# First stage of a fused adaLN, gated delta rule and mixture-of-experts block: groups pipelined, modulation rows spread by TensorE, first weights loaded there

## The chip, the cores and the metric

One core of a Trainium2 chip runs the whole program in one launch. The metric is device time in microseconds, the median of a few runs; smaller is better.

## The reference, cut to what matters

```python
mod = (silu(c) @ wmod).reshape(8, 6, 1, 256)           # sa, ca, ga, sb, cb, gb
h = layernorm(x) * (1 + ca) + sa                       # x: 8 x 256 x 256
x = x + ga * attn(h)                                   # gated delta rule, 32 heads
x = x + gb * ffn(layernorm(x) * (1 + cb) + sb)         # 8 experts, 2 of them per token, and a shared one
# inside attn, first lines:
h = rmsnorm(h, rms1_w)
g = -exp(A_log) * softplus(h @ Wa + dt_bias)           # decay of each head and token
beta = sigmoid(h @ Wb)
q, k, v = conv+silu of h @ Wq, h @ Wk, h @ Wv
```

`ga` and `gb` are kept at least 0.25 away from zero, sign kept. Everything is float32 at the boundaries.

## The kernel before

The program has three parts, one after the other, each a block of its own that all engines enter and leave together: `prepare` (the first stage), `delta_rule` (64 turns, one per batch and group of four heads, software-pipelined by a table of pieces called `PLAN`), and the experts. The change touches `prepare` and the start of `delta_rule`.

**`prepare`.** The 2048 tokens are 16 tiles of 128 rows, in 4 groups of 4 tiles (`GROUPS`, `GT`). SyncE issues all loads (L186 to L196). When every small load has landed (one semaphore, `ld`), ScalarE takes silu of `c`, TensorE makes all six modulation rows for the 8 batches (L221: 6 matmuls, `p_wmod`), VectorE copies them out of PSUM (L293), adds 1 to the scales and bounds the gates (L295 to L303). SyncE stores the rows to memory (L200) and loads two of them back, each copied to all 128 partitions (L202, `p_modb`). VectorE waits for that load and for all of `x`, and then `turn(g)` runs for the four groups in a loop, on all engines in step: mean and variance (L310, L313), the power of -1/2 on GpSimd (L254), centring (L318), times scale and plus shift (L324, into `acc`), squares and their sums on ScalarE (L267), mean of squares, again a power on GpSimd (L256), scaling into `p_hn` (L335), eight transposes on TensorE (L229), and two copies on ScalarE into `hT` (L271), which `delta_rule` reads. VectorE goes to group g+1 only after it has scaled group g.

After the loop TensorE multiplies all of `hT` by `Wa` and `Wb` (L239, 16 matmuls; the four groups write four different ranges of 32 partitions), and a chain of VectorE and ScalarE instructions on tiles of 128 x 512 makes decay and beta: bias (L343), softplus by a series (L344 to L355), the product with exp(A_log) (L357), exp (L281), the reciprocal for beta (L361), running products (L365), a memset (L368). SyncE stores decays (L206) and products (L210) and waits until they have landed; then the stage ends.

**`delta_rule`, start.** SyncE loads `Wo` (L477) and `gnorm_w` (L478), waits for five memsets of VectorE and GpSimd (`set_ok`; L841 to L843, L1003 to L1005), loads the first weights (L487 to L496) and then the tiles of the first two turns: `dr_hb` (L524), `dr_abc` (L525), `dr_bcb` (L528). TensorE waits for `Wo`, the weights and `dr_hb`, and starts with the projections (L593). From there on the table sets the order on every engine.

Of the kernel before, what the change touches and what calls it, by code (L numbers as in the profile page):

```python
# [140 lines left out]

def prepare(nc, A, mem, scr):

    with ExitStack() as ctx:
# [4 lines left out]
        modb = sb("modb", [P, B, 2 * D])  # L149
# [4 lines left out]
        sgn = sb("sgn", [B, 6 * D])  # L154
# [17 lines left out]
        ld, ldx, mod_st, modb_ld, scr_st = (sem(n) for n in ("ld", "ldx", "mod_st", "modb_ld", "scr_st"))
        c_silu, mod_ps, mod_ok = (sem(n) for n in ("c_silu", "mod_ps", "mod_ok"))
        dve, half_ok = (sem(n) for n in ("dve", "half_ok"))
        var_ok, rstd_ok, h0_ok, ss_ok, ms_ok, rr_ok, hn_ok, tr_ps, ht_ok = (
            sem(n) for n in ("var_ok", "rstd_ok", "h0_ok", "ss_ok", "ms_ok", "rr_ok", "hn_ok", "tr_ps", "ht_ok"))
        z_ps, absz_ok, u_ok, sp_ok, a_ok, az_ok, eb_ok, beta_ok, bt_ps, bcum_ok = (
            sem(n) for n in ("z_ps", "absz_ok", "u_ok", "sp_ok", "a_ok", "az_ok", "eb_ok", "beta_ok", "bt_ps", "bcum_ok"))
        acts, done, late, passed, passed_pool = (sem(n) for n in ("acts", "done", "late", "passed", "passed_pool"))
        NLD = 1 + 1 + 2 + 1 + 2 * GROUPS + 1  # L180
# [4 lines left out]
        def _(sp):  # L185
            sp.dma_start(mem["const"][:], A["consts"]).then_inc(ld, 16)  # L186
            sp.dma_start(ct[:], A["c"]).then_inc(ld, 16)
            sp.dma_start(wmod[:], A["wmod"].rearrange("(k p) n -> p k n", k=KT)).then_inc(ld, 16)
            sp.dma_start(wab[:, :, 0:H], A["Wa"].rearrange("(k p) n -> p k n", k=KT)).then_inc(ld, 16)
            sp.dma_start(wab[:, :, H:2 * H], A["Wb"].rearrange("(k p) n -> p k n", k=KT)).then_inc(ld, 16)  # L190
            sp.dma_start(w1c[:], A["rms1_w"]).then_inc(ld, 16)
            for g in range(GROUPS):
                sp.dma_start(dtb[H * g:H * (g + 1), :], A["dt_bias"].rearrange("(h a) -> h a", a=1)).then_inc(ld, 16)
                sp.dma_start(alog[H * g:H * (g + 1), :], A["A_log"].rearrange("(h a) -> h a", a=1)).then_inc(ld, 16)
            for g in range(GROUPS):
                sp.dma_start(x1[:, g * GT:(g + 1) * GT, :],  # L196
                             A["x"].rearrange("b (c p) d -> p (b c) d", p=P)[:, g * GT:(g + 1) * GT, :]).then_inc(ldx, 16)
# [6 lines left out]
            sp.wait_ge(az_ok, 1)  # L204
            for g in range(GROUPS):
# [1275 lines left out]
```

## Time and profile before

| | us |
|---|---|
| median of 3 runs | 2630.22 |
| lowest, highest | 2629.96, 2634.56 |
| the profiled execution, its own time | 2633.98 |
| its span | 2632.2 |

Busy shares of the span: TensorE 94% (weight loads beside it 78%), VectorE 78%, ScalarE 64%, GpSimd 34%. The mean clock granted to TensorE is 0.967 of full speed. The busy share in 40 equal slices (65.8 us each), TensorE above, the granted clock below:

```
PE   1289999999999999999999999999999999789997
PEclk6589999999999999999999999999999999889998
```

A 9 is 90% or more. The profile gives all times from the span's start; names that begin with `p_` belong to `prepare`, with `dr_` to `delta_rule`.

### The profile page before, as it was taken

The numbers are of one execution on the slowest core, as the hardware profiler recorded it, in microseconds if no ns is written. First come the engines' busy times: TensorE is split into PE (matmuls) and PEld (weight loads), VectorE is DVE, ScalarE is ACT, GpSimd is POOL, SyncE is SP. The second block draws the span as 40 slices with busy tenths as digits, with TensorE's granted clock in tenths as the row PEclk, the third lists the DMA queues.
The fourth block names the chain that finished last, engine by engine and source line by source line (L and its number), as shares of the span: only waits on it lengthen the run. The fifth ranks groups of instructions, "written<-read, shape, count | busy, mean of one in ns | idle before, by whom it ended". The sixth has DMA issues, their size and how long they took to land. (4 is left out here: it accounts for less than half of the span.)

```text
span 2632.2 us, 59594 instructions
## 1 busy us (share of the span) xinstructions
PE 2466.6 (94%) x21984; PEld 2063.6 (78%) x21984; DVE 2057.6 (78%) x4303; ACT 1689.0 (64%) x3890; POOL 899.0 (34%) x1053
## 2 busy tenths in 40 slices
PE   1289999999999999999999999999999999789997
PEld 0168888888888888888888888888888888646655
DVE  3468888888888888888888888888888888535444
ACT  1157777777777777777777777777777777522221
POOL 0033444444444444444444444444444444100000
PEclk6589999999999999999999999999999999889998
DMA  2221121112111211121112111121112110031000
GB/s 98 86 57 40 41 60 42 41 41 60 42 41 42 60 41 41 42 60 41 42 41 56 45 42 41 52 49 42 41 45 56 41 42 14 1 121 32 33 6 11
DMA packets 148317, 120.45 MB, mean 46 GB/s; under 512 B 24305, under 2 KB 128698, under 8 KB 148034
## 3 DMA queue, kind: packets, MB, share of 16 engines
q1 hardware_dynamic: 148034, 116.66, 16.7%
q8 instruction: 180, 2.95, 0.5%
q14 instruction: 103, 0.84, 0.1%
HBM read 72.11 MB, written 2.54 MB: 28 GB/s over the span
## 5 line engine op out<-in xcount | busy, mean ns | idle before, releaser
L740 DVE TENSOR_TENSOR dr_w<-dr_ps,mask 128x512 bf16<-128x512 f32 x768 | 526.3, 685 | 90.5 <-PE dr_ps L556 89.7
L754 DVE SCALAR_TENSOR_TENSOR dr_y<-dr_ps,dr_cw,dr_y 128x255 f32<-128x255 f32 (+2 forms) x1152 | 475.8, 474 | 38.1 <-ACT dr_y L870 38.1
L856 ACT CAST dr_tn<-dr_ps 128x512 bf16<-128x512 f32 x640 | 375.0, 586 | 157.6 <-PE dr_ps L569 156.7
L859 ACT CAST dr_tt<-dr_ps 128x512 bf16<-128x512 f32 x768 | 459.2, 598 | 20.9 <-PE dr_ps L576 20.9
L653 PE MATMUL dr_ps<-dr_w,dr_am 128*128 128x96 f32 x3072 | 418.2, 279 | 9.5 <-ACT dr_w L916 2.1
L653 PEld LDWEIGHTS dr_ps<-dr_w,dr_am 128*128 128x128 f32 x3072 | 378.8, 193 | 32.3 <-ACT dr_w L916 24.5
L870 ACT ACTIVATE dr_y<-dr_ps,dr_cw 128x256 f32<-128x256 f32 x384 | 160.9, 470 | 222.2 <-PE dr_ps L593 222.1
L576 PE MATMUL dr_ps<-dr_tt,dr_w 128*128 128x128 bf16 x3072 | 297.6, 219 | 0.9 <-DVE dr_w L740 0.9
L556 PE MATMUL dr_ps<-dr_tn,dr_b 128*128 128x128 bf16 x3072 | 297.6, 219 | 0.0
L982 POOL TENSOR_SCALAR_AFFINE_SELECT dr_b<-dr_b 128x512 bf16<-128x512 bf16 x128 | 81.6, 637 | 506.9 <-ACT dr_b L906 506.9
L569 PEld LDWEIGHTS dr_ps<-dr_w,dr_tt 128*128 128x128 bf16 x2560 | 186.7, 101 | 84.5 <-issue 49.3
L569 PE MATMUL dr_ps<-dr_w,dr_tt 128*128 128x128 bf16 x2560 | 248.5, 220 | 4.2 <-DVE dr_w L740 3.2
L969 POOL TENSOR_TENSOR dr_dg<-const,dr_gam 128x512 f32<-128x512 f32 x128 | 130.4, 1039 | 335.0 <-DVE dr_gam L781 335.0
L916 ACT COPY dr_w<-dr_ps 128x384 f32<-128x384 f32 x384 | 190.0, 495 | 56.8 <-PE dr_ps L653 56.7
L593 PE MATMUL dr_ps<-dr_hb,dr_wqk 128*128 128x256 f32 x768 | 197.0, 393 | 21.1 <-DMA dr_hb<-hT 21.1
L961 POOL TENSOR_TENSOR dr_sq<-dr_sy 128x256 f32<-128x256 f32 x128 | 75.7, 612 | 390.8 <-ACT dr_sy L884 390.8
L576 PEld LDWEIGHTS dr_ps<-dr_tt,dr_w 128*128 128x128 bf16 x3072 | 203.5, 98 | 1.5 <-DVE dr_w L740 1.4
L556 PEld LDWEIGHTS dr_ps<-dr_tn,dr_b 128*128 128x128 bf16 x3072 | 204.4, 98 | 0.0
L719 PE MATMUL dr_ps<-dr_wo,dr_oT 128*128 128x256 f32 x768 | 196.7, 393 | 1.0 <-ACT dr_oT L942 1.0
L614 PE MATMUL dr_ps<-dr_wg,dr_hb 128*128 128x384 f32 x512 | 193.6, 501 | 0.6 <-ACT dr_gs L896 0.6
L789 DVE TENSOR_TENSOR dr_am<-dr_ps,dr_dec 128x512 f32<-128x512 f32 x256 | 174.8, 684 | 24.6 <-PE dr_ps L636 24.5
L766 DVE TENSOR_TENSOR_SCAN dr_dec<-dr_abc,dr_dg 128x512 f32<-128x512 f32 x128 | 191.0, 1492 | 1.3 <-POOL dr_dg L969 1.2
(188 smaller groups left out, 4784.2 us busy)
## 6 DMA issues: line engine op xcount, KB each, us to landing
dr_abc<-scr_a SPq DMA_DIRECT2D x64, 512.0 KB, 5.6
dr_qk<-dr_sy SPq DMA_DIRECT2D x384, 48.0 KB, 2.0
dr_hb<-hT SPq DMA_DIRECT2D x64, 256.0 KB, 2.5
dr_bcb<-scr_b SPq DMA_DIRECT2D x128, 64.0 KB, 4.7
dr_qk<-dr_sy SPq DMA_DIRECT2D x128, 32.0 KB, 1.9
ex_modb<-scr_mod SPq DMA_DIRECT2D x4, 1024.0 KB, 8.2
dr_wo<-in_Wo SPq DMA_DIRECT2D x1, 3072.0 KB, 10.9
dr_wv<-in_Wv SPq DMA_DIRECT2D x8, 384.0 KB, 4.0
```

The costliest lines, as they stand in the source:

```text
L556: last = pe.matmul(ps[:, (X0, X1)[g], (u % QH) * P:(u % QH + 1) * P], b16[:, m, u, :], id16[:] if l == 0 else tn[:, u, :], start=True, sto ...
L569: last = pe.matmul(ps[:, (X2, X1)[g], (u % QH) * P:(u % QH + 1) * P], tt[:, u, :], w16[:, u, :], start=True, stop=True)
L576: last = pe.matmul(ps[:, (X0, X2)[g], (u % QH) * P:(u % QH + 1) * P], wt[:, u, :], id16[:] if l == 0 else tt[:, u, :], start=True, stop=True)
L593: last = pe.matmul(ps[:, BANK[n], j * T:(j + 1) * T], wt, hb[:, m, k, :], start=(k == 0), stop=(k == KT - 1))
L614: last = pe.matmul(ps[:, A0, 0:QV], hb[:, m, k, c * P:(c + 1) * P], wg[:, k, :], start=(k == 0), stop=(k == KT - 1))
L653: last = pe.matmul(ps[:, bank, h * DV:(h + 1) * DV], wt(h), x[:, h * DV:(h + 1) * DV], start=(start and h == 0), stop=(h == QH - 1), skip_ ...
L719: last = pe.matmul(ps[:, CO, 0:D], oT[:, t, :], wo[:, (it // B) * VT + t, :], start=(t == 0), stop=(t == VT - 1))
L740: v.tensor_tensor((tn if l == 0 else w16)[:, us, :], ps[:, (X0, X1)[g], :].rearrange("p (u n) -> p u n", u=QH), bc(mask[:, l, :], 1, QH), ...
L754: v.scalar_tensor_tensor(y[:, slot, x:T], ps[:, BANK[n], off:off + T - x], cw[:, t, TAPS - 1 - x:TAPS - x], y[:, slot, x:T], ALU.mult, ALU ...
L766: v.tensor_tensor_scan(flat(dec[:, us, :]), flat(abc[:, m, c]), flat(dg[:, us, :]), 0.0, ALU.mult, ALU.add).then_inc(s["dec_ok"], 1)
L856: act.copy(tn[:, us, :], ps[:, (X2, X1)[g], :].rearrange("p (u n) -> p u n", u=QH)).then_inc(s["tn_ok"], 1)
L859: act.copy(dst, ps[:, (X0, X2)[g], :].rearrange("p (u n) -> p u n", u=QH)).then_inc(s["tt_ok"], 1)
```

## The change

In `prepare`:

- SyncE loads `c` and the first third of `wmod` first, then `x` (a semaphore for each group), then the constants of the stage, the rest of `wmod`, the first turn's weights (a new function `load_weights`), `gnorm_w` and `Wo`. Those tiles and their semaphores now live for the whole program. At the stage's end it stores decays, products, and last the modulation rows.
- TensorE makes only the first two modulation rows at first (2 matmuls). `spread(b)` copies the two rows of batch b to all partitions by a matmul of a one-hot column with the 8 x 512 rows, into one of three PSUM banks; VectorE multiplies and adds straight from there. The store and the load back are gone from the start.
- The centring moves from VectorE to ScalarE (`center`, Identity with scale and bias; GpSimd makes the bias by one more product). GpSimd scales two of a group's four tiles, VectorE the other two. The squares wait for one another.
- The groups are written out, each engine in an order of its own: VectorE takes the statistics of group g+2 before it is done with group g. `Wa` and `Wb` follow each group (4 matmuls) in place of 16 at the end.
- The other four modulation rows are made after the last group, the gates bounded at the very end on VectorE; the reciprocal for beta comes after the running products.

In `delta_rule` SyncE issues neither weights nor `Wo`: after `set_ok` its first transfer is `dr_hb`. The pieces keep their order on every engine.

```diff
 @block.sync
-            sp.dma_start(mem["const"][:], A["consts"]).then_inc(ld, 16)
-            sp.dma_start(ct[:], A["c"]).then_inc(ld, 16)
-            sp.dma_start(wmod[:], A["wmod"].rearrange("(k p) n -> p k n", k=KT)).then_inc(ld, 16)
+            sp.dma_start(ct[:], A["c"]).then_inc(s["c_ld"], 16)
+            sp.dma_start(wmod[:, :, 0:2 * D], w_v[:, :, 0:2 * D]).then_inc(s["c_ld"], 16)
...
+            sp.dma_start(wmod[:, :, 2 * D:], w_v[:, :, 2 * D:]).then_inc(s["m_ld"], 16)
+            load_weights(sp, A, mem, 0)
+            sp.dma_start(mem["gw"][:], A["gnorm_w"]).then_inc(mem["c_ld"], 16)
+            sp.dma_start(mem["wo"][:], A["Wo"].rearrange("(t p) n -> p t n", p=P)).then_inc(mem["c_ld"], 16)
-            sp.wait_ge(mod_ok, 2)
-            sp.dma_start(scr["mod"], mod[:]).then_inc(mod_st, 16)
-            sp.wait_ge(mod_st, 16)
-            sp.dma_start(modb[:], scr["mod"][:, 0:2 * D].partition_broadcast(P)).then_inc(modb_ld, 16)
...
+            sp.wait_ge(s["mod_ok"], 2)
+            sp.dma_start(scr["mod"], mod[:]).then_inc(s["mod_st"], 16)
+            sp.wait_ge(s["mod_st"], 16)
+            sp.wait_ge(mem["scr_st"], 2 * GROUPS * 16)
 @block.tensor
+            def spread(b):
+                wait(pe, s["bc_free"], b - NBC + 1)
+                pe.matmul(ps[:, BC + b % NBC, :], bc(const[0:B, C_ID + b], 1, P), mod[:, 0:2 * D],
+                          start=True, stop=True).then_inc(s["bc_ps"], 1)
...
+            for g in range(GROUPS):
+                turn(g)
+                steps(g)
+                for b in (2 * g + 4, 2 * g + 5):
+                    if b < B:
+                        spread(b)
 @block.vector
+            stats(0)
+            stats(1)
+            modulate(0)
+            stats(2)
+            means(0)
+            modulate(1)
+            scaled(0)
...
 delta_rule, @block.sync
-            sp.dma_start(wo[:], A["Wo"].rearrange("(t p) n -> p t n", p=P)).then_inc(s["c_ld"], 16)
-            sp.dma_start(gw[:], A["gnorm_w"]).then_inc(s["c_ld"], 16)
-
             sp.wait_ge(s["set_ok"], 5)
+            sp.wait_ge(s["scr_st"], 16 * 2 * GROUPS)
...
-            weights(0)
             batch(0, 0)
             batch(0, 1)
```

TensorE in `prepare`, before. `p_wmod` are the modulation matmuls, `p_hn` the transposes, `p_wab` the products with `Wa` and `Wb`:

```order
L221 MATMUL p_ps<-p_wmod,p_cs 8x512 x6
L229 MATMUL p_ps<-const,p_hn 128x128 x8
...
L229 MATMUL p_ps<-const,p_hn 128x128 x8
L105 REGISTER_ALU
L105 COMPARE_AND_BRANCH
L239 MATMUL p_ps<-hT,p_wab 32x512 x16
L244 MATMUL p_ps<-const,p_t_b 128x128 x4
```

And with the change, where `p_mod,const` are the spreads:

```order
L227 MATMUL p_ps<-p_wmod,p_cs 8x512 x2
L233 MATMUL p_ps<-p_mod,const 128x512 x4
L242 MATMUL p_ps<-const,p_hn 128x128 x8
L250 MATMUL p_ps<-hT,p_wab 32x512 x4
L233 MATMUL p_ps<-p_mod,const 128x512 x2
...
L242 MATMUL p_ps<-const,p_hn 128x128 x8
L250 MATMUL p_ps<-hT,p_wab 32x512 x4
L227 MATMUL p_ps<-p_wmod,p_cs 8x512 x4
L274 MATMUL p_ps<-const,p_t_b 128x128 x4
```

The 16 matmuls of `p_wab` are now four sets of 4, each behind its group's transposes, and eight spreads lie between the groups.

SyncE at the start of `delta_rule`, before:

```order
L477 DMA dr_wo<-in_Wo 128x24x256
L478 DMA dr_gw<-in_gnorm_w 128x3
L487 DMA dr_wqk<-in_Wq 128x2x192
...
L496 DMA dr_cw<-in_conv_v_w 128x3x4
L524 DMA dr_hb<-hT 128x2x256
L525 DMA dr_abc<-scr_a 128x2x512
```

And with the change, from the end of `prepare`:

```order
L210 DMA scr_a<-p_t_a 32x4x128 x4
L215 DMA scr_b<-p_t_bc 32x2x128 x4
L219 DMA scr_mod<-p_mod 8x1536
L153 UNCONDITIONAL_BRANCH
L557 UNCONDITIONAL_BRANCH
L593 DMA dr_hb<-hT 128x2x256
L594 DMA dr_abc<-scr_a 128x2x512
```

Eleven transfers have left the place between the two stages, and the store of the modulation rows has come to the end of the first.

## Rows read from the trace of the kernel before

**Rows 1.** Busy time by stretches: first stage, the gap, the rest.
```profile
0.00:112.94 112.94, 21.87 (x80) 9.52 (x80) 54.41 (x131) 17.04 (x47) 8.36 (x13) 0.63 0.18 61
112.94:128.58 15.64, 0.00 (x0) 0.03 (x1) 1.30 (x3) 0.00 (x0) 0.18 (x3) 0.50 0.98 316
128.58:2632.20 2503.62, 2444.75 (x21904) 2054.07 (x21904) 2001.93 (x4169) 1671.97 (x3843) 890.44 (x1037) 0.99 0.17 43
```

The columns are: stretch, its length, busy time and instructions of PE, PEld, DVE, ACT, POOL, granted clock, DMA share, GB/s.

**Rows 2.** Timeline up to the first group (start, length, engine, line).
```profile
11.87 7.36 PE L221 MATMUL p_ps<-p_wmod,p_cs 128*8 128x512 f32 x12 [11.87 <-ACT p_cs L263]
...
24.28 0.35 SPq L200 DMA_DIRECT2D scr_mod<-p_mod  x1
26.38 0.38 SPq L202 DMA_DIRECT2D p_modb<-scr_mod  x1
33.24 1.41 DVE L310 BATCH_NORM_STATS2 p_st<-p_x 128x6 f32<-128x256 f32 x4 [8.99 <-DMA p_modb<-scr_mod]
```

**Rows 3.** Timeline of the second group and the start of the third.
```profile
44.70 1.40 DVE L310 BATCH_NORM_STATS2 p_st<-p_x 128x6 f32 x4
...
49.69 2.73 DVE L324 TENSOR_TENSOR acc<-acc,p_modb  x4 [0.17 <-DVE acc L318]
52.55 0.42 ACT L267 ACTIVATE p_sq<-acc 128x256 f32 x1 [5.02 <-DVE acc L324]
...
55.68 1.14 DVE L335 TENSOR_SCALAR p_hn<-acc,p_rr 128x256 f32 x4 [1.22 <-POOL p_rr L256]
56.73 1.40 DVE L310 BATCH_NORM_STATS2 p_st<-p_x 128x6 f32 x4
```

**Rows 4.** Busy time by stretches, as rows 1, around TensorE's bursts.
```profile
20.00:44.00 24.00, 0.00 (x0) 0.00 (x0) 10.50 (x31) 1.70 (x8) 2.02 (x2) 0.56 0.24 89
80.00:84.00 4.00, 2.08 (x12) 1.69 (x16) 0.91 (x4) 1.53 (x3) 0.00 (x0) 0.50 0.00 0
87.00:90.00 3.00, 2.41 (x20) 0.48 (x15) 1.97 (x4) 0.85 (x2) 0.00 (x0) 0.88 0.00 0
```

**Rows 5.** Timeline, the last transposes and the products with `Wa` and `Wb`.
```profile
81.04 1.96 PE L229 MATMUL p_ps<-const,p_hn 128*128 128x128 f32 x8 [10.09 <-DVE p_hn L335]
...
83.88 5.53 PE L239 MATMUL p_ps<-hT,p_wab 128*32 128x512 f32 x32 [0.87 <-ACT hT L271]
```

**Rows 6.** Timeline of the first stage's end.
```profile
87.64 0.75 DVE L343 TENSOR_SCALAR p_t_z<-p_ps,p_dtb 128x512 f32<-128x512 f32 x1 [6.73 <-PE p_ps L239]
...
102.97 3.35 DVE L361 RECIPROCAL p_t_b<-p_t_q 128x512 f32<-128x512 f32 x1
106.24 1.31 DVE L365 TENSOR_TENSOR_SCAN p_t_bc<-p_t_a,p_t_zero 128x128 f32<-128x128 f32 x4
...
112.94 0.10 POOL L1003 MEMSET dr_half<- 128x8 f32 x1 [33.21 <-POOLq L144]
```

**Rows 7.** Timeline of the gap between the stages.
```profile
113.39 4.98 SPq L478 DMA_DIRECT2D dr_gw<-in_gnorm_w  x1
...
114.50 0.06 DVE L843 MEMSET dr_mso<- 128x4 f32 x1
...
124.53 0.71 SPq L524 DMA_DIRECT2D dr_hb<-hT  x1
...
128.58 4.56 PE L593 MATMUL dr_ps<-dr_hb,dr_wqk 128*128 128x256 f32 x12 [21.09 <-DMA dr_hb<-hT]
...
136.63 3.92 SPq L509 DMA_DIRECT2D dr_qk<-dr_sy  x6
```

**Rows 8.** DMA issues up to 120 us: size, median us from issue to landing.
```profile
const<-in_consts SPq DMA_DIRECT2D x1, 528.0 KB, 3.5
```

**Rows 9.** The page's DMA issues, the same columns.
```profile
dr_abc<-scr_a SPq DMA_DIRECT2D x64, 512.0 KB, 5.6
...
dr_hb<-hT SPq DMA_DIRECT2D x64, 256.0 KB, 2.5
```

**Rows 10.** The page's groups: GpSimd on a 128 x 256 tile.
```profile
L961 POOL TENSOR_TENSOR dr_sq<-dr_sy 128x256 f32<-128x256 f32 x128 | 75.7, 612 | 390.8 <-ACT dr_sy L884 390.8
```

More of the change, by code:

```diff
@@ L216, in _, with modulation @@
         def _(pe):
-            pe.wait_ge(ld, 16 * NLD + 0)
-            pe.wait_ge(c_silu, 1)
-            for n in range(3):
+            def modulation(n, bank):
                 for k in range(KT):
-                    last = pe.matmul(ps[0:B, n, :], cs[:, k, :], wmod[:, k, n * 512:(n + 1) * 512],
+                    last = pe.matmul(ps[0:B, bank, :], cs[:, k, :], wmod[:, k, n * 512:(n + 1) * 512],
                                      start=(k == 0), stop=(k == KT - 1))
-            last.then_inc(mod_ps, 1)
+                return last
@@ L242, in _, with steps @@
-            pe.wait_ge(beta_ok, 1)
+                        last = pe.transpose(ps[:, TR + k, j * P:(j + 1) * P], hn[:, g % 2, j, k * P:(k + 1) * P],
+                                            const[:, C_ID:C_ID + P])
+                    last.then_inc(s["tr_ps"], 1)
+            def steps(g):
+                pe.wait_ge(s["ht_ok"], (g + 1) * KT)
+                for w in range(2):
+                    for k in range(KT):
+                        last = pe.matmul(ps[H * g:H * (g + 1), (ZA, ZB)[w], :], wab[:, k, H * w:H * (w + 1)],
+                                         hT[:, k, g * GTOK:(g + 1) * GTOK], start=(k == 0), stop=(k == KT - 1))
+                    last.then_inc(s["z_ps"], 1)
@@ new lines, in _ @@
+            pe.wait_ge(s["c_ld"], 32)
+            pe.wait_ge(s["c_silu"], 1)
+            modulation(0, TMP).then_inc(s["mod_ps"], 1)
+            pe.wait_ge(s["id_ld"], 16)
+            pe.wait_ge(s["modr_ok"], 2)
+            for b in range(4):
+                spread(b)
+            pe.wait_ge(s["k_ld"], 16 * NK)
+            for g in range(GROUPS):
[3 more added lines that the diff above has]
+                    if b < B:
+                        spread(b)
@@ L258, in _, with center @@
-            groups(pool, turn)
+            pool.memset(nh[:], -0.5).then_inc(s["half_ok"], 1)
+            pool.wait_ge(s["half_ok"], 1)
+            def center(g):
+                gs = slice(g * GT, (g + 1) * GT)
+                pool.wait_ge(s["var_ok"], (g + 1) * 2)
+                pool.tensor_tensor(rstd[:, gs], var[:, gs], nh[:], ALU.pow).then_inc(s["rstd_ok"], 1)
+                pool.wait_ge(s["rstd_ok"], g + 1)
+                pool.tensor_tensor(nmr[:, gs], nmean[:, gs], rstd[:, gs], ALU.mult).then_inc(s["nmr_ok"], 1)
@@ new lines, in _ @@
+            center(0)
+            center(1)
+            squares(0)
+            center(2)
+            act.wait_ge(s["k_ld"], 16 * NK)
+            turn(0)
+            squares(1)
+            center(3)
+            turn(1)
+            squares(2)
+            turn(2)
+            squares(3)
+            turn(3)
+            act.activation(ea[:], alog[:], ACT.Exp).then_inc(s["ea_ok"], 1)
+            act.wait_ge(s["az_ok"], 1)
+            act.activation(tmp["u"][:], tmp["az"][:], ACT.Exp, scale=-1.0).then_inc(s["u_ok"], 1)
@@ L338, in _ @@
[L338 to L346 removed]
+            c = Chain(v, s["late"])
+            v.wait_ge(s["k_ld"], 16 * NK)
```

340 lines of the change are left out of this document (177 added, 163 removed).

## The prediction

> **What bounds the kernel now.** I read the windows first. From 128.58 us on TensorE is busy for 2444.75 of 2503.62 us at a granted clock of 0.99; the change leaves the order of that part alone on every engine, so nothing is to be won or lost there unless its instructions get longer. Ahead of it lie 128.58 us in which TensorE works for 21.87 us: a first stage of 112.94 us and a gap of 15.64 us [rows 1]. There no engine is full (VectorE 54.41 us); the time is a chain of waits. The timeline shows four pieces of it. (a) Up to 33.24: the loads, six modulation matmuls, a store issued at 24.28 whose landing lets the load back go at 26.38, and that load's landing, on which VectorE's first statistics wait [rows 2]. (b) Four groups, one after the other, 12.03 us apart (44.70 to 56.73), since VectorE, ScalarE, GpSimd and TensorE hand one group round [rows 3]. (c) From the bias at 87.64 to the next stage's first instruction at 112.94: 25.30 us, nearly all one VectorE chain [rows 6]. (d) The gap: SyncE is held by the issue of `gnorm_w` behind `Wo` to 118.37, issues the weights, and only at 124.53 `dr_hb`, for which TensorE waits to 128.58 [rows 7].
>
> **The change, part by part.** I lay out the new stage on the same clock.
>
> *Start.* `c` and 512 KB of `wmod` are issued by 1.6. The first load now, of 528 KB, landed 3.5 us after its issue [rows 8], so I put TensorE's start at 5.4 instead of 11.87; it could be 7, should `x` behind it share the engines. A matmul of 512 columns is two passes. The last products ran as 8 sets of 4 passes side by side, 3.8 us of them before the grant rose at 87.7 and 1.7 us after [rows 4, 5]: 0.86 a set at the low level (1.2 GHz) and 0.43 at the high one (2.4 GHz). The 12 passes in 7.36 us [rows 2] fit the same two values, 5 and 7 of them. Two matmuls are four passes, at the low level 3.4 us: 8.8. Two copies of 8 x 256 out of PSUM, at most the 0.75 of a 128 x 512 read there [rows 6]: 9.8 with the handovers. Store and load back are off the path; their data come by eight spreads, two passes each.
>
> *First group.* Statistics 1.4 and 0.6 for the rest: 11.8. The power on GpSimd keeps VectorE idle for 1.22 [rows 3]; the product on 128 x 4 behind it no row shows: between nothing and the power's 1.2, I take 0.3, since it is one multiplication of four columns. Four centrings on ScalarE by the nearest row, a square of the same size at 0.42 [rows 3], at most 0.75: 1.7. That gives 15.0. Four multiplications and additions are 2.73 from SBUF [rows 3]; from PSUM I take the same, 17.1. The next group's centring covers that, then four squares that wait for each other, 0.56 each: 19.1. Mean and power 1.4; GpSimd's two tiles 0.61 each [rows 10], beside VectorE, which first modulates group 1: the first transposes go at 22.9. In the kernel before they could go when VectorE came free for group 1, at 44.70 [rows 3].
>
> *Groups.* Here the engines overlap, and the question is what the longest chain is. Per group TensorE has eight transposes, 1.96; then, after ScalarE's copies, 2.84 from the transposes' start to the products [rows 5]; eight passes for `Wa` and `Wb`; four for two spreads. Before, the 32 passes took 5.53 us [rows 5], less than the 13.8 that 32 at 0.43 would take: four ran side by side, one for each 32 output partitions. Written per group they follow one another, so all 32 cost 13.8 at the high level and 27.5 at the low one. That is the price of this part, and the spreads join the path: modulate(2) and modulate(3) need spreads 4 to 7, which lie behind steps(0) and steps(1).
>
> The grant decides. Before, it was 0.50 through the transposes and rose at 87.7, 3.9 us after the products began (0.88 of 87 to 90); after the first burst, over at 19.2, it fell at 22.9 (0.56 of 20 to 44) [rows 4]. So steps(0), from 26.4 on, starts low and turns high at about 30; with two spreads it ends at 33.4. VectorE multiplies (the first while the second spread runs), adds and scales in 2.8: transposes of group 1 at 36.3. From there I take the high level: +10.6 to group 2 (2.6 to the products, 3.4, 1.7, then 2.9), +7.4 to group 3, which waits for no spread but for squares, mean, power and scaling: 54.3. Products at 57.0, the first half 1.7 to 3.4 us: the bias goes at about 60, and I write 60.5 for the handovers. Against 87.64: **27.1 us less**.
>
> *Tail.* The chain to exp is the same. The reciprocal for beta moves behind the scans: exp of the decay ends 15.6 after the bias, scans 1.31 [rows 6], memset, 17.1; reciprocal 3.35, 20.4; then the new gate chain on VectorE, one addition and four operations on 8 x 512, priced by their 128 x 512 forms (0.42 to 0.69): 23.1. SyncE's store of the rows then takes the 2.1 us that it took at 24.28 [rows 2], and the barrier 0.5: 25.7 where it was 25.3. **0.4 us more.** The stores of decays and products, issued from 17.1 on, are covered by the reciprocal. The four late modulation matmuls and ScalarE's copy of 8 x 1024 have 12 us before ScalarE needs to be free for the exp: nothing. The stage ends at 86.2.
>
> *Gap.* `Wo` and weights are 30 us old by then. VectorE's memsets end 1.6 us after the stage (114.56 against 112.94), `dr_hb` is issued at once and lands in 2.5 [rows 7, 9]: TensorE starts 4.3 us into the gap instead of 15.64. **11.3 us less.** What is late next: `dr_abc` is issued 0.7 us after `dr_hb`, lands 5.6 later [rows 9], and is needed by the scan some 14 us into the turn. SyncE issues the next batch when these have landed, about 9 to 11.5 into the gap, and the gathers of `dr_qk` wait behind that: they went 8.05 us after TensorE's start [rows 7], so at 12.4. It just fits. Cost nothing; without that room at most 3.
>
> *Sum.* 27.1 - 0.4 + 11.3 = 38.0 us off the profiled execution: 2633.98 to 2596.0. That execution stands 3.8 us above the median of its runs; I forecast the median and take the same 38 off 2630.22: **2592 us**. Unknown costs: the start 1.6 us later; centring at 0.75, 1.3 us in the first group; the clock one burst earlier or later, 2 us each way.
>
> **A rule against it.** The rows show that the grant stayed at 0.50 through the last burst of transposes [rows 4]. The Trainium skill, TensorE: Matmul & The Clock Gate, Part 4, says that transposes do not count as TensorE being busy in the way matmuls do; by that rule the trace agrees, and the stretches between the new groups' products would look idle. What the stage would be then is the first rival. The skill's page SBUF — State Buffer, Who interferes with whom, adds that GpSimd and a VectorE instruction with two SBUF inputs block each other; the rows before show no such pair in this stage. By that page each of GpSimd's scalings could wait for one VectorE instruction: an estimate of 0.7 us a group, 2 to 3 in all, 2594 to 2595.
>
> **Rivals.**
> 1. *The grant stays low in the stage.* Each set of eight passes then costs 6.9, each two spreads 3.4, half of the last products 3.4. Group 1's transposes go at 39.4, group 2's at 55.2, group 3's at 64.9 (TensorE busy with steps(2) until then), the bias at 71.1: 10.6 us lost, 2603. For it: bursts of 5 to 7 us with 3 us between them, and the low grants of the stretches shown [rows 4]. Against: the bursts are denser than any in the stage before. 0.17.
> 2. *The gap is not freed.* TensorE starts early but the turn then waits for `dr_abc` or for gathers behind the next batch on SyncE, or `dr_hb` lands in 4 us as the first one did (124.53 to 128.58) [rows 7]. 4 to 6 us lost, 2597. For it: 1 us of room. Against: the first `dr_hb` had 1.2 MB of weights ahead of it. 0.12.
> 3. *Slower.* The weight tiles leave the delta rule's memory and all its tiles move. Should the placement lengthen what TensorE reads there, it would show one for one, since TensorE has no room [rows 1]. With 64 turns the point of decision is 0.6 us a turn; at 1 us a turn it gives 2656. Nothing in the rows shows any effect of placement. 0.03.
> 4. *It does nothing*: the turns' start-up absorbs the earlier start. TensorE's fill is paced by its own first pieces, which start earlier as a whole. 0.01.
>
> **How the numbers follow.** Forecast 0.67. Its own range: start 5 to 7, clock, gap 3.5 to 6, and the run's own spread of 4.6 us around: 2586 to 2598. Rivals 1 and 2 lie above and are taken in; 3 is left out: 2586 to 2604. A measurement here can tell 0.2%, 5.3 us; all but rivals 3 and 4 are faster by more: faster 0.96, same 0.01, slower 0.03.
>
> **What would show it.** First transposes at about 23; bias instruction at 57 to 64; stage end near 86; first projections 4 to 5 us later; from there on the same length as the 2503.62 us now, give or take 3. Wrong if: the bias comes after 70, or windows between 26 and 57 read 0.50 throughout (rival 1); the first scan or the key transposes wait for DMA (rival 2); the time from the first projection to the end differs by over 5 us (rival 3 or a different start of the clock in the first turns).

## The result, and the profile after

| | before | after |
|---|---|---|
| median, run side by side | 2632.31 | 2594.28 |
| lowest, highest | 2629.96, 2634.56 | 2592.89, 2595.21 |
| the profiled execution, its span | 2633.98, 2632.2 | 2592.89, 2590.9 |

The ratio is 0.9855, with a 95% interval from 0.9838 to 0.9872: 38.0 us less, as forecast, with an interval of 34 to 43. The median is 2.3 us above the 2592 of the prediction, 2.1 of it because the kernel before came out at 2632.31 where the prediction started from 2630.22. The two profiled executions stand 41.3 us apart in span. The windows split that, cut at the same places as [rows 1] (the columns too):

```profile
0.00:87.31 87.31, 42.01 (x96) 13.90 (x96) 45.84 (x107) 26.77 (x64) 14.00 (x25) 0.73 0.34 104
87.31:91.62 4.31, 0.00 (x0) 0.03 (x1) 1.30 (x3) 0.00 (x0) 0.18 (x3) 0.50 0.25 87
91.62:2590.90 2499.28, 2439.88 (x21904) 2051.01 (x21904) 2002.03 (x4169) 1673.30 (x3843) 891.50 (x1037) 0.99 0.17 44
```

The first stage is 25.6 us shorter, the gap 11.3, and the rest 4.3 with the same 21904 matmul passes. GpSimd does more in the stage (14.00 us for 8.36), VectorE less (45.84 for 54.41).

The timeline of the stage's start and first group, which answers to [rows 2]:

```profile
5.14 3.57 PE L227 MATMUL p_ps<-p_wmod,p_cs 128*8 128x512 f32 x4 [5.14 <-ACT p_cs L309]
...
9.42 1.38 DVE L366 BATCH_NORM_STATS2 p_st<-p_x 128x6 f32<-128x256 f32 x4
...
12.83 4.04 ACT L315 ACTIVATE acc<-p_x,p_nmr,p_rstd 128x256 f32<-128x256 f32 x8 [7.83 <-POOL p_nmr L288]
...
22.77 1.94 PE L242 MATMUL p_ps<-const,p_hn 128*128 128x128 f32 x8 [4.37 <-DVE p_hn L398]
```

The first statistics start at 9.42 instead of 33.24, and the first transposes at 22.77. Before, they stood at 44.84 and those of the last group at 81.04:

```profile
44.84 1.97 PE L229 MATMUL p_ps<-const,p_hn 128*128 128x128 f32 x8 [25.60 <-DVE p_hn L335]
```

The four groups and the bias, answering to [rows 3] and [rows 5]:

```profile
26.30 5.02 PE L250 MATMUL p_ps<-hT,p_wab 128*32 128x512 f32 x8 [1.59 <-ACT hT L328]
...
31.25 1.98 PE L233 MATMUL p_ps<-p_mod,const 8*128 8x512 f32 x4
...
32.48 0.69 DVE L379 TENSOR_TENSOR acc<-acc,p_ps 128x512 f32<-128x512 f32 x1 [3.84 <-PE p_ps L233]
...
35.61 0.61 DVE L398 TENSOR_SCALAR p_hn<-acc,p_rr 128x256 f32<-128x256 f32 x2
36.28 1.97 PE L242 MATMUL p_ps<-const,p_hn 128*128 128x128 f32 x8 [3.05 <-DVE p_hn L398]
...
39.03 5.48 PE L250 MATMUL p_ps<-hT,p_wab 128*32 128x512 f32 x8 [0.78 <-ACT hT L328]
...
49.55 1.93 PE L242 MATMUL p_ps<-const,p_hn 128*128 128x128 f32 x8 [3.13 <-DVE p_hn L398]
52.26 5.69 PE L250 MATMUL p_ps<-hT,p_wab 128*32 128x512 f32 x8 [0.78 <-ACT hT L328]
...
57.88 1.09 PE L242 MATMUL p_ps<-const,p_hn 128*128 128x128 f32 x8
...
61.91 0.75 DVE L421 TENSOR_SCALAR p_t_zz<-p_ps,p_dtb 128x512 f32<-128x512 f32 x1 [4.09 <-PE p_ps L250]
```

The groups follow each other 13.51, 13.27 and 8.33 us apart. That is 35.1 us for three spacings where the kernel before needed 36.2 (44.84 to 81.04): pipelined as it is, the middle of the stage is hardly shorter. The row at 32.48 shows why: VectorE's first multiplication for group 2 waits 3.84 us for a spread, which stands behind steps(0), and VectorE's scaling of group 1 stands behind that multiplication in its own order, so it runs at 35.61, though the power that it needs was done at 29.73. (steps(g) is the set of eight passes for `Wa` and `Wb` of group g, L250.) The first three sets of eight passes take over 5 us each; for the second and third 3.4 at the high level was forecast. The granted clock, in windows around them:

```profile
30.00:40.00 10.00, 6.17 (x18) 2.64 (x16) 3.28 (x6) 4.35 (x10) 2.16 (x4) 0.80 0.00 2
40.00:50.00 10.00, 6.87 (x15) 1.93 (x14) 3.45 (x7) 1.02 (x4) 2.19 (x3) 0.84 0.00 0
50.00:60.00 10.00, 8.30 (x24) 3.15 (x24) 2.26 (x5) 4.71 (x13) 2.24 (x3) 0.68 0.00 1
```

One more thing is new: VectorE and GpSimd scale the fourth group's tiles at the same moment. The timeline of VectorE's scaling in the third group and of both in the fourth:

```profile
48.88 0.62 DVE L398 TENSOR_SCALAR p_hn<-acc,p_rr 128x256 f32<-128x256 f32 x2 [0.22 <-DVE acc L383]
...
55.72 1.43 DVE L398 TENSOR_SCALAR p_hn<-acc,p_rr 128x256 f32<-128x256 f32 x2 [1.12 <-POOL p_rr L293]
55.77 1.23 POOL L298 TENSOR_TENSOR p_hn<-acc,p_rr 128x256 f32<-128x256 f32 x2
```

The stage's end and the gap, answering to [rows 6] and [rows 7]:

```profile
87.31 0.10 POOL L1071 MEMSET dr_half<- 128x8 f32 x1 [30.32 <-POOLq L153]
...
88.94 0.71 SPq L593 DMA_DIRECT2D dr_hb<-hT  x1
...
91.62 5.46 PE L661 MATMUL dr_ps<-dr_hb,wqk 128*128 128x256 f32 x12 [8.08 <-DMA dr_hb<-hT]
...
100.81 6.49 SPq L578 DMA_DIRECT2D dr_qk<-dr_sy  x10
...
106.57 1.97 DVE L834 TENSOR_TENSOR_SCAN dr_dec<-dr_abc,dr_dg 128x512 f32<-128x512 f32 x1 [1.22 <-POOL dr_dg L1037]
```

Nothing of the weights stands before `dr_hb` any more. The first scan waits for GpSimd, not for `dr_abc`.

### The profile page after: what moved, and what is told of

It is laid out like the page before. It is cut to its first block and busy times, and to the rows that moved or that the text cites. A ratio compares the mean times of both kernels' runs of the same rounds, so it can differ in the third digit from the quotient of the medians.

```text
span 2590.9 us, 59545 instructions
## 1 busy us (share of the span) xinstructions
PE 2481.9 (96%) x22000; PEld 2064.9 (80%) x22000; DVE 2049.2 (79%) x4279; ACT 1700.1 (66%) x3907; POOL 905.7 (35%) x1065
## 5 line engine op out<-in xcount | busy, mean ns | idle before, releaser
L822 DVE SCALAR_TENSOR_TENSOR dr_y<-dr_ps,cw,dr_y 128x255 f32<-128x255 f32 (+2 forms) x1152 | 475.7, 473 | 27.1 <-ACT dr_y L938 27.1
L938 ACT ACTIVATE dr_y<-dr_ps,cw 128x256 f32<-128x256 f32 x384 | 161.3, 471 | 209.9 <-PE dr_ps L661 209.7
L661 PE MATMUL dr_ps<-dr_hb,wqk 128*128 128x256 f32 x768 | 197.1, 393 | 8.1 <-DMA dr_hb<-hT 8.1
L787 PE MATMUL dr_ps<-wo,dr_oT 128*128 128x256 f32 x768 | 197.2, 393 | 1.0 <-ACT dr_oT L1010 1.0
L682 PE MATMUL dr_ps<-wg,dr_hb 128*128 128x384 f32 x512 | 192.9, 500 | 0.6 <-ACT dr_gs L964 0.6
```

Of the source, the lines that this page charges most:

```text
L661: last = pe.matmul(ps[:, BANK[n], j * T:(j + 1) * T], wt, hb[:, m, k, :], start=(k == 0), stop=(k == KT - 1))
L682: last = pe.matmul(ps[:, A0, 0:QV], hb[:, m, k, c * P:(c + 1) * P], wg[:, k, :], start=(k == 0), stop=(k == KT - 1))
L787: last = pe.matmul(ps[:, CO, 0:D], oT[:, t, :], wo[:, (it // B) * VT + t, :], start=(t == 0), stop=(t == VT - 1))
L822: v.scalar_tensor_tensor(y[:, slot, x:T], ps[:, BANK[n], off:off + T - x], cw[:, t, TAPS - 1 - x:TAPS - x], y[:, slot, x:T], ALU.mult, ALU ...
```

## The experiments

All medians are in microseconds, each with the kernel before run beside it on the same chip; that one's medians are 2632.31 to 2635.25 over the sets, and the change's own two are 2594.28 and 2595.62 (experiment 9). So a difference of a few microseconds between medians of different sets shows little, and the steps inside the stage are read from the traces. Where a distance to the change is given, it is to 2594.28. The theory, called A in the expectations: the gain is the sum of the shorter stage and the shorter gap, each one for one. Each expectation spells out what A means for its run.

**1. The change without the early weights.** `Wo`, `gnorm_w` and the first weights go back behind the stage's end.

```diff
 prepare, @block.sync
-            load_weights(sp, A, mem, 0)
-            sp.dma_start(mem["gw"][:], A["gnorm_w"]) ...
-            sp.dma_start(mem["wo"][:], A["Wo"] ...
 delta_rule, @block.sync
+            sp.dma_start(wo[:], A["Wo"] ...
+            sp.dma_start(gw[:], A["gnorm_w"]) ...
...
+            load_weights(sp, A, mem, 0)
             batch(0, 0)
```

> The changed kernel with Wo, gnorm_w and the first weights loaded where they were before. Theory A (the gap of 15.64 us was only the wait for these transfers, and the earlier start comes through whole): first stage as in the changed kernel, its end at 87.3 us, first projections 15.6 us later, total 11.3 us more than the changed kernel, 27 less than before. Theory B (the delta rule's start-up takes most of it back: first turns wait for dr_abc and for the gathers): 0 to 5 us more than the changed kernel. What the clock grants in the first turns may move either by 4 us.

Measured: 2610.97 against 2634.38, ratio 0.9921 (0.99 to 0.9943). The timeline of its gap:

```profile
87.25 0.40 SPq L556 DMA_DIRECT2D wo<-in_Wo  x1
87.71 4.98 SPq L557 DMA_DIRECT2D gw<-in_gnorm_w  x1
...
98.84 0.71 SPq L593 DMA_DIRECT2D dr_hb<-hT  x1
...
102.94 5.11 PE L662 MATMUL dr_ps<-dr_hb,wqk 128*128 128x256 f32 x12 [19.46 <-DMA dr_hb<-hT]
```

The stage ends at 87.24, as with the change, and the gap is back at 15.70 us. SyncE stands 4.98 us on the issue of `gnorm_w` right behind `Wo`; in the changed kernel, ahead of `Wo`, the same issue took 0.49. So the early weights are worth 11.4 us in the trace, as theory A says. The median is 16.7 us above the change's, 5 us more than the gap explains and more than theory A with its 4 us of clock allowed: two runs lie at 2606 and 2607, among them the profiled one, and two at 2615. Why these two are longer is not shown.

**2. The kernel before with the early weights alone.** The same three lines, put behind the load of `p_modb`.

```diff
             sp.dma_start(modb[:], scr["mod"][:, 0:2 * D].partition_broadcast(P)).then_inc(modb_ld, 16)
+            load_weights(sp, A, mem, 0)
+            sp.dma_start(mem["gw"][:], A["gnorm_w"]).then_inc(mem["c_ld"], 16)
+            sp.dma_start(mem["wo"][:], A["Wo"].rearrange("(t p) n -> p t n", p=P)).then_inc(mem["c_ld"], 16)
```

> The kernel before with only the early loads, issued behind the load of the spread modulation rows, nothing else changed. Theory A: first stage ends at 112.9 as before, first projections 4.3 us later, 11.3 us less than before (about 2620). Theory B: less than 5 us won. Also possible: the 4.4 MB slow the load of the modulation rows; they are issued behind it, so no.

Measured: 2623.16 against 2634.38, ratio 0.9965 (0.9952 to 0.9978), 11.2 us less. The bias stands at 88.28, 0.6 later than before, the stage ends at 113.59, and TensorE starts 4.32 us after that:

```profile
113.59 0.10 POOL L1003 MEMSET dr_half<- 128x8 f32 x1 [33.22 <-POOLq L160]
115.22 0.71 SPq L525 DMA_DIRECT2D dr_hb<-hT  x1
...
117.91 4.27 PE L593 MATMUL dr_ps<-dr_hb,wqk 128*128 128x256 f32 x12 [9.78 <-DMA dr_hb<-hT]
```

Each part of the change works without the other. In the traces the stage is 25.7 us shorter alone (experiment 1) and the gap 11.3 (here), against 25.6 and 11.3 with both, so they add up there. The medians give 23.4 and 11.2, together 34.6, which is 3.4 short of 38.0 and inside what the two intervals allow.

**3. The rows through memory again.** Everything else of the change is kept, and the two rows are stored, loaded back to all partitions, and VectorE reads them from SBUF.

```diff
 prepare, @block.sync, behind the small loads
+            sp.wait_ge(s["modr_ok"], 2)
+            sp.dma_start(scr["modr"], mod[:, 0:2 * D]).then_inc(s["mod_st"], 16)
+            sp.wait_ge(s["mod_st"], 16)
+            sp.dma_start(modb[:], scr["modr"].partition_broadcast(P)).then_inc(s["bc_ps"], 16)
 @block.tensor
-            for b in range(4):
-                spread(b)
...
-                for b in (2 * g + 4, 2 * g + 5):
-                    if b < B:
-                        spread(b)
```

> The changed kernel with the two modulation rows stored and loaded back for all partitions instead of spread by TensorE; all else as changed. Theory A (the spreads save the round trip at the start and cost their place between the groups): first multiplication at 21 instead of 14, first transposes near 30; but the later groups wait for no spread, 9 to 10 us apart instead of 13: bias at about 62, total within 3 us of the changed kernel. Theory C (the spreads are the main gain of the stage): 7 to 9 us more.

Measured: 2592.45 against 2634.38, ratio 0.9855 (0.9833 to 0.9877): the change's own ratio. Its timeline, from the store of the rows to the bias:

```profile
11.89 0.37 SPq L205 DMA_DIRECT2D scr_modr<-p_mod  x1
...
22.11 1.29 DVE L379 TENSOR_TENSOR acc<-acc,p_modb 128x512 f32<-128x512 f32 x2 [8.73 <-DMA p_modb<-scr_modr]
...
30.96 1.94 PE L247 MATMUL p_ps<-const,p_hn 128*128 128x128 f32 x8 [22.10 <-DVE p_hn L398]
...
62.26 0.75 DVE L421 TENSOR_SCALAR p_t_zz<-p_ps,p_dtb 128x512 f32<-128x512 f32 x1 [3.41 <-PE p_ps L255]
```

As theory A says, the bias is at about 62 and the total within 3 us of the change. The spreads bring the first transposes 8.2 us forward, and by the bias only 0.35 of that is left. Without spreads on TensorE the groups lie 10.1, 10.3 and 7.0 us apart instead of 13.5, 13.3 and 8.3: no multiplication of VectorE waits for a spread that waits for products, and no scaling stands behind such a multiplication. The spread by TensorE, as placed, is worth nothing that the runs can tell. What makes the start early all the same is that two rows are made from a third of `wmod`, stored here at 11.89 instead of 24.28 [rows 2], and that statistics and centring don't wait for them; neither of the two was taken away alone.

**4. The groups in step.** The change with the order of the kernel before.

```diff
 @block.vector
-            stats(0)
-            stats(1)
-            modulate(0)
...
+            for g in range(GROUPS):
+                stats(g)
+                modulate(g)
+                means(g)
+                scaled(g)
```

ScalarE and GpSimd are written in step in the same way.

> The changed kernel with the groups taken in step: statistics, centring, modulation, squares, mean and scaling of one group before the next on VectorE, ScalarE and GpSimd. Theory A (from the trace: groups are 13.5, 13.3 and 8.3 us apart with the pipeline, 12.0 before it, so running ahead bought about nothing once the products and spreads lie between the groups): groups about 13.3 apart, bias at 65 to 66 instead of 61.9, 3 to 5 us more. Theory D (running ahead is what shortened the stage): groups 16 or more apart, 10 us more.

Measured: 2598.22, ratio 0.9869 (0.985 to 0.9887), 3.9 us above the change. Transposes at 23.22, 34.92, 46.72 and 58.47, the bias at 63.84:

```profile
33.44 1.42 DVE L388 TENSOR_SCALAR p_hn<-acc,p_rr 128x256 f32<-128x256 f32 x2 [1.12 <-POOL p_rr L293]
...
34.92 1.10 PE L242 MATMUL p_ps<-const,p_hn 128*128 128x128 f32 x8 [1.91 <-DVE p_hn L388]
...
36.93 6.49 PE L250 MATMUL p_ps<-hT,p_wab 128*32 128x512 f32 x8 [0.92 <-ACT hT L326]
...
39.25 0.69 DVE L369 TENSOR_TENSOR acc<-acc,p_ps 128x512 f32<-128x512 f32 x1 [2.52 <-ACT acc L313]
...
63.84 0.75 DVE L400 TENSOR_SCALAR p_t_zz<-p_ps,p_dtb 128x512 f32<-128x512 f32 x1 [4.76 <-PE p_ps L250]
```

In step the first three groups even follow faster, 11.7 us apart, than pipelined, 13.5. The written-out order is worth 1.9 us at the bias; theory A had 3 to 4, with groups 13.3 apart, and the groups came out closer than that. In step the path between two groups does not run through TensorE: its spreads are done before VectorE multiplies, VectorE waits 2.52 us for ScalarE's centring (39.25) and never for a spread, and TensorE waits for the scaling (1.91 at 34.92). In the change it does run through TensorE, by the wait at 32.48 and what stands behind it on VectorE. In step VectorE and GpSimd also scale at the same moment in all four groups, 1.42 us each time where 0.61 is usual, and here the transposes wait for it: by subtraction some 3 us over the four groups.

**5. The spreads ahead of the products.** One line moved.

```diff
                 turn(g)
-                steps(g)
                 for b in (2 * g + 4, 2 * g + 5):
                     if b < B:
                         spread(b)
+                steps(g)
```

> The changed kernel with the two spreads between the groups issued ahead of the group's products instead of behind them; their PSUM banks are free since 17 and 22 us. Theory A (the spreads are late only because they stand behind the products, so products and spreads lie on the path from group to group): second and third transposes near 32 and 42 instead of 36.3 and 49.6, bias at 54 to 57 instead of 61.9, total 5 to 8 us less than the changed kernel. Theory E (the path runs through squares and powers anyhow): 0 to 2 us less.

Measured: 2588.69 against 2634.8, ratio 0.9824 (0.9808 to 0.9841), 5.6 us below the change; its four runs (2588.24 to 2590.79) all lie below the eight of the change (2592.89 and more). The spacings fall to 11.75, 7.89 and 6.96, the bias stands at 53.59, 8.3 earlier:

```profile
28.54 6.24 PE L250 MATMUL p_ps<-hT,p_wab 128*32 128x512 f32 x8
34.71 1.10 PE L242 MATMUL p_ps<-const,p_hn 128*128 128x128 f32 x8
...
53.59 0.75 DVE L421 TENSOR_SCALAR p_t_zz<-p_ps,p_dtb 128x512 f32<-128x512 f32 x1 [3.42 <-PE p_ps L250]
```

**6. The products last, side by side.** Per group only transposes and spreads; the 16 products after the loop, the four groups' output partitions in turn, as before the change.

```diff
                 turn(g)
-                steps(g)
...
+            pe.wait_ge(s["ht_ok"], GROUPS * KT)
+            for w in range(2):
+                for g in range(GROUPS):
+                    for k in range(KT):
+                        last = pe.matmul(ps[H * g:H * (g + 1), (ZA, ZB)[w], :], wab[:, k, H * w:H * (w + 1)],
+                                         hT[:, k, g * GTOK:(g + 1) * GTOK], start=(k == 0), stop=(k == KT - 1))
```

> The changed kernel with all products with Wa and Wb behind the last group, four side by side as before the change, and the spreads right behind the transposes. Theory A: groups about 9 us apart, last transposes near 50, the products start 2.8 later and the bias 3.8 after that (low level), at 56 to 57: 5 us less than the changed kernel, and 1 to 2 more than spreads first with products per group. Theory F (products per group are what saved time at the end): bias at 60 or later.

Measured: 2587.41, ratio 0.9827 (0.9811 to 0.9844), 6.9 us below the change and not to be told from experiment 5.

```profile
49.37 1.97 PE L242 MATMUL p_ps<-const,p_hn 128*128 128x128 f32 x8 [5.72 <-DVE p_hn L404]
52.12 5.19 PE L271 MATMUL p_ps<-hT,p_wab 128*32 128x512 f32 x32 [0.78 <-ACT hT L334]
...
55.74 0.75 DVE L427 TENSOR_SCALAR p_t_zz<-p_ps,p_dtb 128x512 f32<-128x512 f32 x1 [5.76 <-PE p_ps L271]
```

All transposes run at the low level here (1.97 for eight), and it costs little, for the products of all four groups together take 5.19 us where the change spends over 5 on each of three. The groups lie 9.3, 9.5 and 7.7 us apart, with each transpose waiting for the scaling. In the trace the bias comes 2.1 us later than in experiment 5; that its profiled execution is 6.0 us shorter all the same (span 2582.8 for 2588.8) lies in the delta rule, which took 2497.3 us here and 2505.3 there.

**7. Dummy matmuls between the groups.** 3, 3, 1 and 0 products of the constants, 128x512, behind each group's spreads: nothing else is altered, TensorE is only kept at work.

```diff
+                for _ in range((3, 3, 1, 0)[g]):
+                    pe.matmul(ps[:, TMP, :], const[:, C_ID:C_ID + P], const[:, 0:512], start=True, stop=True)
```

> The changed kernel with 3, 3 and 1 dummy float32 matmuls of 512 columns behind the spreads of groups 0 and 1 and the products of group 2, into a PSUM bank that nothing reads then. Theory A (products 1 and 2 ran at the low level because TensorE was idle between groups; the trace has them at 5.5 and 5.7 us against 3.4 at the high level): grant stays high from 30 on, products 3.4 to 3.6, bias at 57 to 59, 3 to 4 us less. Theory G (the gaps are not what lets the grant fall): products as before, and the dummies push the transposes back by 1 to 2 us each.

Measured: 2593.54, ratio 0.9845 (0.9828 to 0.9861). Steps(1) and steps(2) take 3.62 us, the high level, instead of 5.48 and 5.69:

```profile
26.36 6.18 PE L250 MATMUL p_ps<-hT,p_wab 128*32 128x512 f32 x8 [1.59 <-ACT hT L330]
...
39.52 3.62 PE L250 MATMUL p_ps<-hT,p_wab 128*32 128x512 f32 x8 [0.92 <-ACT hT L330]
...
50.19 3.62 PE L250 MATMUL p_ps<-hT,p_wab 128*32 128x512 f32 x8 [0.92 <-ACT hT L330]
...
59.17 0.75 DVE L423 TENSOR_SCALAR p_t_zz<-p_ps,p_dtb 128x512 f32<-128x512 f32 x1 [3.41 <-PE p_ps L250]
```

Transposes stand at 22.84, 37.50, 48.18 and 55.14: the last two spacings are 10.68 and 6.96 instead of 13.27 and 8.33. The first is 14.66, for steps(0) took 6.18 here, ahead of any dummy, where the change's took 5.02. The bias stands 2.7 us earlier than with the change, and theory A had 3 to 4 for the total. The level was what made groups 2 and 3 late; the median is 0.7 below the change's, too near to show it.

**8. Dummy matmuls ahead of the delta rule.** Two behind the transposes of beta, two at the head of TensorE's `delta_rule`.

```diff
 prepare, behind the transposes of beta
+            for _ in range(2):
+                pe.matmul(ps[:, ZA, :], const[:, C_ID:C_ID + P], const[:, 0:512], start=True, stop=True)
 delta_rule, ahead of the first piece
+            for _ in range(2):
+                pe.matmul(ps[:, CO, :], const[:, C_ID:C_ID + P], const[:, 0:512], start=True, stop=True)
```

> The changed kernel with two dummy matmuls behind the beta transposes at the end of the first stage and two ahead of the first projections, so that TensorE is busy from 83.6 to about 91 with nothing waiting for it. Theory A (the low grant at the start of the delta rule costs what its projections take longer): first twelve projection passes 4.1 us instead of 5.5, first turn 1 to 2.5 us shorter, total 1 to 3 us less. Theory H (the later drops of the grant in the first turns decide, and fall where they fall): no difference beyond the spread of runs.

Measured: 2592.62, ratio 0.9838 (0.9821 to 0.9854).

```profile
92.54 2.83 PE L663 MATMUL dr_ps<-dr_hb,wqk 128*128 128x256 f32 x12 [2.23 <-DMA dr_hb<-hT]
```

The first twelve passes take 2.83 us instead of 5.46, and still the time from there to the end is 2499.5, against 2499.3. What is gained at once is given back in this profile: the next two sets of four passes with `wg` take 2.91 and 2.93, where the change's took 2.91 and 1.56, and the fourth issue of `dr_hb` comes 41.3 us after the first projections and not 38.7. The median, 1.7 below the change's, does not part the two theories.

**9. The change once more**, not altered.

> The change once more, not altered, to tell how far one profiled execution of one kernel moves. Theory (the granted clock in the first turns of the delta rule falls out differently from execution to execution): stage end within 0.5 us of 87.3 and the gap 4.3 again, but the time from the first projections to the end, 2499.3 in the first profile, may come out anywhere from 2497 to 2505. Rival (that time belongs to the program, and its 4.3 us below the kernel before are a lasting gain of the earlier start): 2499.3 again, within 1 us. Median 2592 to 2595.

Measured: 2595.62, ratio 0.9854 (0.9837 to 0.987). Bias at 62.22, gap 4.3; from the first projections (91.94) to the end of the span (2593.8) 2501.9 us, against 2499.3 in the first profile. So this part moved by 2.6 us between two profiles of one kernel. Over the thirteen profiles of this case, of twelve kernels with the delta rule's pieces and their order the same in each, it is 2497.3 to 2505.3, with the kernel before at 2503.6. So the 4.3 us gained there in the first pair of profiles are not shown to be an effect of the change. Between the longest and the shortest, most of the difference had come by the fourth issue of `dr_hb`: 43.0 us after the first projections in experiment 5 (2505.3 to the end), 37.1 in experiment 6 (2497.3). It is no rule for all: experiment 1 had 43.1 there and 2501.4 to the end.

**10. Spreads first, with too many dummy matmuls.** Experiment 5 and 18 dummies behind the first spreads, 2, 1, 1 and 0 behind the products.

> The run with the spreads ahead of the products (bias at 53.59), and besides 18 dummy matmuls of the constants (128x512) behind the first four spreads and 2, 1, 1, 0 behind the groups' products. In that run steps(0) took 6.24 us, part of it at the low level, and TensorE reached group 1's transposes only when it was done. Theory (TensorE's level sets the first spacing): steps(0) takes 3.6 us, transposes at about 23, 33, 41, 47.5, bias at 51.5 and stage end near 77, 2 us earlier than there; over the whole kernel 2586 to 2589, since the level in the first turns moves the rest by up to 8 us between runs. Rival (the fillers only take TensorE's time, and the spacing of 11.7 us is set by squares, means and powers): bias stays at 53.5 or comes later.

Measured: 2598.58, ratio 0.9866 (0.985 to 0.9883), slower than experiment 5, with the bias at 64.89 where 51.5 was expected. The miss is one of my own count: one such matmul is two passes, about 1 us, and 18 of them held TensorE until 36.65. The groups then followed 8.24, 9.02 and 6.95 us apart, with each of the first three sets of products at 3.62.

**11. Fewer of them.** 2 behind the third spread, 4 behind the fourth, 1 behind each of the first two groups' products.

> The run with the spreads ahead of the products (bias at 53.59), with fewer dummy matmuls than the last: 2 behind the third spread and 4 behind the fourth, 1, 1, 0, 0 behind the groups' products. In the last run 18 of them held TensorE until 36.65, 13.7 us too long; its groups then followed 8.24, 9.02 and 6.95 us apart, with 4.03 to the bias. Theory (what is left in the first spacing is TensorE's level, and the last run lost only by my count): the dummies end by 22, first transposes near 23, steps(0) 3.6 us, bias at 23 + 24 + 4 = 51, give or take 1; stage end 76.5. Rival (the groups of the last run were close only because VectorE and ScalarE had 14 us to get ahead): bias at 53.5 as without dummies. Median 2586 to 2590 by the theory, 2588 to 2592 by the rival: the medians won't part them, the bias will.

Measured: 2588.94 against 2635.25, ratio 0.9832 (0.9819 to 0.9846).

```profile
26.34 5.06 PE L250 MATMUL p_ps<-hT,p_wab 128*32 128x512 f32 x8 [0.55 <-ACT hT L332]
...
35.71 5.32 PE L250 MATMUL p_ps<-hT,p_wab 128*32 128x512 f32 x8 [0.48 <-ACT hT L332]
...
52.85 0.75 DVE L425 TENSOR_SCALAR p_t_zz<-p_ps,p_dtb 128x512 f32<-128x512 f32 x1 [3.41 <-PE p_ps L250]
```

The first transposes run at the high level (1.07), but steps(0) and steps(1) are partly low again, and the bias comes at 52.85: 0.7 earlier than in experiment 5 and not the 51 expected. Both theories missed. With these dummies the low stretch stood in another place and was not gone. Over the whole kernel this is experiment 5 (2588.69) with needless work in it.

## Why the prediction was right, point by point

- **Start.** Forecast: TensorE's start at 5.4, first transposes at 22.9. Measured: 5.14 and 22.77. One centring took 0.51 where a square's 0.42 was assumed (4.04 for eight), GpSimd's product 0.20 where 0.3 was.
- **Group 1.** Forecast: steps(0) from 26.4, spreads done at 33.4, transposes at 36.3. Measured: 26.30, 33.23, 36.28. The chain was the right one, down to the rise of the level inside steps(0).
- **Groups 2 and 3: the step that failed.** "From there I take the high level" was wrong. The level fell again between the bursts (0.80, 0.84 and 0.68 of three windows), steps(1) took 5.48 and steps(2) 5.69 for the forecast 3.4, and the spacings were 13.27 and 8.33 for 10.6 and 7.4: group 3's transposes at 57.88 for 54.3, 3.6 us late. Experiment 7 shows the cause: with dummy work between the groups the same products take 3.62 and the spacings are 10.68 and 6.96.
- **From the last transposes to the bias.** Forecast 6.2, measured 4.03: the level had risen inside steps(2), so the transposes took 1.09 and the products came 2.01 us behind their start where 2.7 was forecast, and the bias 2.02 behind that, where up to 3.4 and some handovers were allowed. This gave 2.2 us back, so that the bias stands at 61.91 against 60.5 and the size of the stage's gain is off by 1.4.
- **Tail.** Forecast 25.7, measured 25.40 (before: 25.30). Scans end at 78.98, 17.07 after the bias, the reciprocal at 82.38, the gates at 84.79, 22.9 after the bias for 23.1: all within about 0.2 us of the steps named.
- **Gap.** Forecast 4.3, measured 4.31; experiments 1 and 2 find 11.4 and 11.2 us for it. The gathers of `dr_qk` went 9.2 us after TensorE's start, 1.1 later than before, and no wait behind them showed: the first scan waited for GpSimd. Rival 2 fell, and by the measured gain so did rival 4.
- **The rest.** Forecast: the same length, give or take 3. Measured 4.3 less in the profiled pair, and 1.7 more to 6.3 less over all profiles. Stage and gap together gave 37.0 us in the traces for the 38.0 forecast, since the stage ended 1.1 us late. That the medians differ by 38.0 to the decimal is luck: their interval is 34 to 43 us, and the turns alone move by more than 1 us.
- **Rival 1** (the grant stays low in the stage) had the mechanism half right. It would have put group 3 at 64.9 and the bias at 71.1; measured 57.88 and 61.91. The rows show a level that rose inside steps(0), steps(1) and steps(2) each time and fell in between. The Trainium skill, TensorE: Matmul & The Clock Gate, Part 4, says that transposes don't count as TensorE being busy in the way matmuls do. The rows can't part that from their small amount of work: in experiment 6, where transposes and spreads stood alone, they stayed at 1.97, and behind products they took 1.09 or 1.97.
- **Rival 3** (placement) fell: the delta rule's 2499.3 us lies below the 2503.6 of before, and it is 2499.6 in experiment 2, where of the whole change only the weights and their tiles moved.
- **The port.** The rows show VectorE's scaling of two tiles at 1.43 us while GpSimd scales the other two, and 0.62 without. The Trainium skill, SBUF — State Buffer, Who interferes with whom, lists `tensor_scalar` among what can take the pair shared with GpSimd; I had drawn on its sentence on two SBUF inputs alone. The estimate of 0.7 us a group came true once, 0.8 us in the last group, and there steps(2) hid it. In the others VectorE scaled after GpSimd was done. In experiment 4 it came in all four groups and nothing hid it. That the port is the reason is the page's account; the rows show only the times.

What I had thought to be the gain's reason was only partly it. Of the 25.7 us at the bias, 22.1 are there at the first transposes (22.77 for 44.84), 1.1 come in the three spacings and 2.6 behind the last transposes. The start itself splits by subtraction of rows, up to the first statistics (9.42 for 33.24, 23.8 us): TensorE starts 6.7 us earlier, two modulation matmuls take 3.8 less than six, their copies 4.3 less than copies and gates did, and 9.0 were the store and the load back, for which the statistics no longer wait. These four were not tested one by one.

The spread by TensorE (experiment 3: 0.35 us) and the pipelining (experiment 4: 1.9 us) are worth little as placed, since each group's spreads wait behind its products, and on VectorE the scaling of the group ahead waits with them. That holds for this placement alone. With the rows through memory the pipelined groups are 10.1, 10.3 and 7.0 us apart, and with the spreads first 11.8, 7.9 and 7.0, where in step they are 11.7, 11.8 and 11.8. With spreads first or products last (experiments 5 and 6) the same parts give 5.6 and 6.9 us more, 2588.69 and 2587.41. In step with the spreads first was not tried.

Open: why experiment 11's low stretches fall where they do. In the profiles of experiments 5, 6 and 7 the recorded grant reads 1.00 up to about 60 us, though transposes there took 1.94 to 1.97, so only durations tell the level. Not tried: letting the store of the modulation rows land behind the stage's end, which could give at most the 1.7 us between the end of beta's copies (85.58) and the stage's end (87.31); their tile would have to outlive the stage.

## What to carry to other kernels

Before pipelining a chain over engines, ask what stands in front of it: loads waited for together, six rows made where two are needed first, and a round trip through memory were 24 us here by the first statistics, out of 26 at the bias, and the order of the groups 2. A pipelined order also has its price: on VectorE the scaling of one group stood 6 us behind a multiplication of the next that waited for TensorE. On an in-order engine put what other engines wait for (here the spreads) ahead of what nobody waits for (the products): one moved line gave 5.6 us. First weights whose tiles can live through the stage before belong into that stage; the gap between two blocks fell from 15.6 to 4.3 us, a few memsets and one small load.

## What the runs showed of the hardware

- Matmuls into four different ranges of 32 output partitions ran side by side: 32 passes of 128x512 took 5.19 to 6.40 us (experiments 6 and 2, the kernel before 5.53), and 8 into one range already 3.62 at the high level (experiment 7).
- Eight 128x128 transposes took 1.94 to 1.97 us at the low level and 1.04 to 1.10 at the high one.
- The issue of one small load (`gnorm_w`) took 4.98 us on SyncE when it came right behind that of `Wo` (the kernel before and experiment 1), and 0.49 where it came ahead of it.
- Two 128x256 scalings on VectorE took 1.42 to 1.43 us while GpSimd scaled two tiles of the same size (in the last group of the change and in all four of experiment 4), and 0.61 to 0.62 without that. GpSimd's two took 1.23 then, and 1.18 to 1.19 otherwise.
- From the first projections to the end, thirteen profiles read 2497.3 to 2505.3 us; the 8 us between them are a fifth of what this change gains. The level is seen to differ in them: the first four passes with `wg` took 1.56 us in experiment 6 and 2.91 in experiment 5. That it makes up all of the 8 us is not shown. Runs of one kernel lay up to 8.9 us apart (experiment 1), so a few microseconds of difference between two spans are no evidence of a change's effect.
